# Splitting the sixteen-chunk layer-norm statistics of a macaron transformer layer into two halves of eight chunks

## The chip, the cores and the metric

The kernel runs on all 8 NeuronCores of one Trainium2 chip, each core with four of the 32 sequences and no exchange between cores. The metric is device time in microseconds (us) of the slowest core. The engines named below are TensorE (PE, its weight loads PEld), VectorE (DVE), ScalarE (ACT), GpSimd (POOL) and SyncE (SP); each works through its own list of instructions in order, and they meet through semaphores.

## The reference

Every sequence is a matrix of 2048 tokens by 1024 features and passes three residual stages, each of which starts with a layer norm without weights:

```
def _layernorm(x, axis=-1, eps=1e-5):
    m = jnp.mean(x, axis=axis, keepdims=True)
    v = jnp.var(x, axis=axis, keepdims=True)
    return (x - m) / jnp.sqrt(v + eps)

x = x + 0.5 * ffn(_layernorm(x), w_gate, w_up, w_down)   # silu(x wg^T) * (x wu^T), then wd^T; hidden 3072
x = x + attn(_layernorm(x), Wq, Wv, Wo, Wg, ...)         # q * ema_scan(v), a second norm, silu gate, Wo
x = x + 0.5 * ffn(_layernorm(x), w_gate, w_up, w_down)
```

The attention stage replaces softmax by a decaying sum over time per head, followed by a norm of its own with gamma and beta.

## The kernel before

One core runs its four sequences one after the other, and in each the phases A (feed-forward), B (attention) and C (the same feed-forward). A sequence stays on the chip as X, 16 chunks of 128 tokens by 1024 features in bf16. Each phase starts with `layer_norm_to_xn`, so the program passes through it 12 times.

The norm has three parts. `ln_stats(c)` takes one chunk's row sum on DVE (L541) and row sum of squares on ACT (L545), into one column of a small table STATS. It is called outside the norm: in A, after chunk c has received its feed-forward result (L680, the last third of the hidden dimension); in B, at the end of `part2(c)` (L853); at the change of sequence, after the next sequence's chunks have been loaded into X: `boundary_cb` stores four chunks and loads four (streams io0 to io3, on POOL), calls `ln_stats` for the four chunks before those, and the last four are called after phase C. Only the very first norm calls all sixteen itself. Then, once for all 16 chunks, come 18 small DVE instructions on 16 columns: mean (L552), its square (L555), variance (L558), and `emit_rsqrt`, an integer first guess of the inverse root and three Newton steps (L521 to L536). Each reads what the one in front of it wrote, and waits for it through DVE's own semaphore. Last, chunk by chunk: DVE subtracts and scales (L566, into one of two buffers TMPTM), PE transposes the result in eight 128x128 pieces into the one PSUM bank PSB7b (L570), ACT copies it to XN (L576). The matmuls that follow read XN: `L608` (gate) and `L635` (up) in A and C, `L718` (projections) in B.

The order on every engine is the order in which the Python code calls `em.op`; nothing reorders it later. `Em` derives the waits: every buffer or statistic has a key (such as `ST_ssum`), a reader waits for the key's last writer, a writer also for its readers, and a wait that an earlier one on the same engine already covers is left out.

Two things around the norm matter. Weights come over SP (stream `wl`): gate and up into WA and WB, later down (L653), and for attention four blocks (L693 to L703). In the first sequence the attention weights are first transposed by 32 DMA transposes (L454) with as many stores (L457), which stand on SP after the last L653 of phase A and ahead of L693. Inside attention `part1b` does the same 18 instructions for one chunk, on one column (L785 to L791, then L521 to L536); the change leaves that alone.

Of the kernel before, what the change touches and what calls it, by code (L numbers as in the profile page):

```python
# [11 lines left out]
ALU = mybir.AluOpType  # L12
AX = mybir.AxisListType
# [4 lines left out]
D = 1024  # L18
# [228 lines left out]
def build_program():  # L247
# [61 lines left out]
    STATS = sb("STATS", [128, 128], F32)  # L309
# [34 lines left out]
    em = Em()  # L344
# [14 lines left out]
    kX = [f"X{c}" for c in range(NCH)]  # L359
# [152 lines left out]
    def stat(namecol, c=None):  # L512
        base = st_cols[namecol]
        if c is None:
            return STATS[:, base:base + 16]
        return STATS[:, base + c:base + c + 1]

    MAGIC = 0x5f3759df

    def emit_rsqrt(varcol, varkey, wcol, wkey, tcol, tkey, zcol, zkey):  # L520
        em.op("vector", lambda v: v.tensor_scalar(wcol, varcol, float(EPS), None, ALU.add),  # L521
              reads=[varkey], writes=[wkey])
        wi, ti, zi = wcol.bitcast(I32), tcol.bitcast(I32), zcol.bitcast(I32)
        em.op("vector", lambda v: v.tensor_scalar(ti, wi, 1, None, ALU.arith_shift_right),
              reads=[wkey], writes=[tkey])
        em.op("vector", lambda v: v.tensor_scalar(zi, ti, -1, MAGIC, ALU.mult, ALU.add),
              reads=[tkey], writes=[zkey])
        for _ in range(3):
            em.op("vector", lambda v: v.tensor_tensor(tcol, zcol, zcol, ALU.mult),
                  reads=[zkey], writes=[tkey])  # L530
            em.op("vector", lambda v: v.tensor_tensor(tcol, tcol, wcol, ALU.mult),
                  reads=[tkey, wkey], writes=[tkey])
            em.op("vector", lambda v: v.tensor_scalar(tcol, tcol, -0.5, 1.5,
                                                      ALU.mult, ALU.add),
                  reads=[tkey], writes=[tkey])
            em.op("vector", lambda v: v.tensor_tensor(zcol, zcol, tcol, ALU.mult),  # L536
                  reads=[zkey, tkey], writes=[zkey])

    def ln_stats(c):
        xc = X[:, D * c:D * (c + 1)]  # L540
        em.op("vector", lambda v, xc=xc, c=c: v.reduce_sum(  # L541
            stat("ssum", c), xc, axis=AX.X), reads=[kX[c]], writes=["ST_ssum"])
        sq = TMPTM[:, D * (c % 2):D * (c % 2 + 1)]
        em.op("scalar", lambda s, xc=xc, c=c, sq=sq:
              s.activation(sq, xc, AF.Square, accum_out=stat("ssq", c)),  # L545
              reads=[kX[c]], writes=["ST_ssq", f"TT{c % 2}"])

    def layer_norm_to_xn(prestats=True):
        if not prestats:
            for c in range(NCH):  # L550
                ln_stats(c)
        em.op("vector", lambda v: v.tensor_scalar(  # L552
            stat("mu"), stat("ssum"), 1.0 / D, None, ALU.mult),
            reads=["ST_ssum"], writes=["ST_mu"])
        em.op("vector", lambda v: v.tensor_tensor(  # L555
            stat("musq"), stat("mu"), stat("mu"), ALU.mult),
            reads=["ST_mu"], writes=["ST_musq"])
        em.op("vector", lambda v: v.scalar_tensor_tensor(  # L558
            stat("var"), stat("ssq"), 1.0 / D, stat("musq"), ALU.mult, ALU.subtract),
            reads=["ST_ssq", "ST_musq"], writes=["ST_var"])  # L560
        emit_rsqrt(stat("var"), "ST_var", stat("sd"), "ST_sd",
                   stat("musq"), "ST_musq", stat("rstd"), "ST_rstd")
        for c in range(NCH):
            xc = X[:, D * c:D * (c + 1)]
            tm = TMPTM[:, D * (c % 2):D * (c % 2 + 1)]
            em.op("vector", lambda v, xc=xc, tm=tm, c=c: v.tensor_scalar(  # L566
                tm, xc, stat("mu", c), stat("rstd", c), ALU.subtract, ALU.mult),
                reads=[kX[c], "ST_mu", "ST_rstd"], writes=[f"TT{c % 2}"])
            bank, bkey = PSB7, "PSB7"
            items = [(lambda t, tm=tm, f=f, bank=bank: t.transpose(  # L570
                bank[:, 128 * f:128 * (f + 1)], tm[:, 128 * f:128 * (f + 1)], IDN[:]),
                [f"TT{c % 2}", "IDN"]) for f in range(KC)]
            em.group("tensor", items, writes=[bkey])
            xnv = XN[:].rearrange("p (f t) -> p f t", t=S)[:, :, 128 * c:128 * (c + 1)]
            bv = bank[:].rearrange("p (f t) -> p f t", t=128)
            em.op("scalar", lambda s, xnv=xnv, bv=bv: s.activation(xnv, bv, AF.Copy),  # L576
                  reads=[bkey], writes=[kXN[f][c] for f in range(KC)])

    def ffn_phase(tap=False, prestats=True, next_stats=True, tail_cb=None,
                  skip_gw0=False):  # L580
        layer_norm_to_xn(prestats=prestats)
        if tap:
            em.dma("st", lambda g: g.dma_start(out=dbg_xn, in_=XN[:]),
                   reads=[k for row in kXN for k in row], writes=["DBGXN"])
        nsl = NSLAB if DBG_SLABS is None else DBG_SLABS
        for j in range(nsl):
# [69 lines left out]
            for c in range(NCH):  # L656
# [20 lines left out]
                if j == NSLAB - 1 or (DBG_SLABS is not None and j == DBG_SLABS - 1):  # L677
                    xc = X[:, D * c:D * (c + 1)]
                    ac = ACC[:, D * c:D * (c + 1)]
                    em.op("vector", lambda v, xc=xc, ac=ac: v.tensor_tensor(  # L680
                        xc, xc, ac, ALU.add),
                        reads=[kX[c], kACC[c][0], kACC[c][1]], writes=[kX[c]])
                    if next_stats:
                        ln_stats(c)
                    if tail_cb is not None:
                        tail_cb(c)
# [3 lines left out]

    def attn_phase():
        layer_norm_to_xn(prestats=True)
        em.dma("wl", lambda s: s.dma_start(  # L693
            out=WA[:].rearrange("p (k h) -> p k h", h=D), in_=scr_a["wq"]),
# [131 lines left out]
        def part2(c):  # L826
# [15 lines left out]
            for n in range(2):  # L842
# [11 lines left out]
                    xc, xc, PSB[bank2][:], ALU.add),  # L854
                    reads=[kX[c], kPSB[bank2]], writes=[kX[c]])
            ln_stats(c)

        for c in range(NCH + 2):
# [21 lines left out]
    for w in ("wq", "wv", "wgt", "wo"):  # L880
# [5 lines left out]
        reads=[f"scrT_wgate_r{r}" for r in range(HID // 128)], writes=["WSLOTA"])  # L886
# [3 lines left out]
        reads=[f"scrT_wup_r{r}" for r in range(HID // 128)], writes=["WSLOTB"])  # L890
# [88 lines left out]
```

How the kernel before makes its waits and increments, by code:

```python
        def body(engobj, eng):  # L225
            waited = {}
            for inst in em.ins[eng]:
                for dep in inst["deps"]:
                    sem, val = resolve(dep)
                    key = id(sem)
                    if waited.get(key, 0) < val:
                        engobj.wait_ge(sem, val)
                        waited[key] = val
                bi = inst["fn"](engobj)
                if inst["stream"] is not None:
                    bi.then_inc(semh[("d", inst["stream"])], 16)
                elif inst["inc"]:
                    bi.then_inc(semh[("e", eng)], 1)
```

## Time and profile before

| what | us |
|---|---|
| median of the 8 runs shown | 7573.2 |
| lowest and highest of them | 7253.7 and 7932.08 |
| profiled execution, its own time | 7256.6 |
| its span (core 6, the slowest) | 7255.1 |
| spans of the 8 cores | 7231.1 to 7255.1 |
| PE busy | 5702.6 (79%) |
| DVE busy | 2082.8 (29%) |
| ACT busy | 1474.9 (20%) |

The page's busy shares are means over stages that differ: PE is nearly always busy in the feed-forward stages, waits in parts of attention, and stands between two phases while a norm is made ready. A change in the norm is therefore read in the stretch of a norm, by what PE waits for there.

### The profile page before, as it was taken

The numbers are of one execution on the slowest core, as the hardware profiler recorded it, in microseconds if no ns is written. First come the engines' busy times: TensorE is split into PE (matmuls) and PEld (weight loads), VectorE is DVE, ScalarE is ACT, GpSimd is POOL, SyncE is SP. The second block draws the span as 40 slices with busy tenths as digits, with TensorE's granted clock in tenths as the row PEclk, the third lists the DMA queues.
The fourth block names the chain that finished last, engine by engine and source line by source line (L and its number), as shares of the span: only waits on it lengthen the run. The fifth ranks groups of instructions, "written<-read, shape, count | busy, mean of one in ns | idle before, by whom it ended". The sixth has DMA issues, their size and how long they took to land.

```text
span 7255.1 us, 81111 instructions; the slowest of 8 cores (7231.1 to 7255.1 us)
## 1 busy us (share of the span) xinstructions
PE 5702.6 (79%) x29138; PEld 2833.1 (39%) x29138; DVE 2082.8 (29%) x3929; ACT 1474.9 (20%) x2342; POOL 173.1 (2%) x112
## 2 busy tenths in 40 slices
PE   0012998685998799786998799786998699786899
PEld 0011444443443344443443344443444344443444
DVE  0012124244123213344123213444123213444123
ACT  1000212222211211322211221322211221322211
POOL 0000000000000000000000000000000000000000
PEclk9999999787999899887999899887999799887899
DMA  8733013200013000100013110100012110100002
GB/s 98 117 97 94 24 47 85 67 1 24 30 41 99 30 35 24 47 1 24 24 47 86 37 41 24 47 1 24 24 45 73 45 47 24 47 1 24 24 35 70
DMA packets 152526, 322.12 MB, mean 44 GB/s; under 512 B 112336, under 2 KB 112336, under 8 KB 140048
## 3 DMA queue, kind: packets, MB, share of 16 engines
q1 hardware_dynamic: 134016, 239.10, 10.0%
q0 software_dynamic: 18128, 77.84, 6.3%
q8 instruction: 252, 4.13, 0.2%
q14 instruction: 130, 1.06, 0.0%
HBM read 291.74 MB, written 88.08 MB: 52 GB/s over the span
## 4 chain that ended last, share of the span: by engine, by line
PE 70%; DVE 9%; DMA 8%; issue 5%; ACT 4%; another core or an unknown queue 3%; DVEq 1%; SPq 0%; ACTq 0%; POOL 0%; POOLq 0%
PE PSB L608 18%; PE PSB L635 18%; PE PSB L660 14%; PE PSB L718 9%; PE PSB L846 5%; PE PSB7b L570 2%; ACT XN L576 2%; DMA TSTB<-nat_g 2%; DVE STATS L541 1%; DMA TSTB<-nat_u 1%; DVE ACC L674 1%; DMA X<-x 1%; DMA o<-X 1%; ACT ACC L839 1%
## 5 line engine op out<-in xcount | busy, mean ns | idle before, releaser
L645 DVE TENSOR_TENSOR H<-SG,PSB 128x512 bf16<-128x512 bf16 x768 | 528.1, 688 | 2620.6 <-PE PSB L635 2620.6
L660 PE MATMUL PSB<-WA,H 128*128 128x512 bf16 x4096 | 892.0, 380 | 32.0 <-DVE ACC L674 32.0
L625 ACT ACTIVATE SG<-PSB 128x512 bf16<-128x512 f32 x768 | 458.6, 597 | 2200.2 <-PE PSB L608 2200.1
L608 PE MATMUL PSB<-XN,WA 128*128 128x512 bf16 x4096 | 902.5, 383 | 0.0
L635 PE MATMUL PSB<-XN,WB 128*128 128x512 bf16 x4096 | 889.3, 379 | 0.0
L660 PEld LDWEIGHTS PSB<-WA,H 128*128 128x128 bf16 x4096 | 401.4, 98 | 520.1 <-issue 40.8
L608 PEld LDWEIGHTS PSB<-XN,WA 128*128 128x128 bf16 x4096 | 403.7, 99 | 491.7 <-issue 17.4
L635 PEld LDWEIGHTS PSB<-XN,WB 128*128 128x128 bf16 x4096 | 401.1, 98 | 482.9
L570 PE MATMUL PSB7b<-IDN,TMPTM 128*128 128x128 bf16 x1536 | 193.9, 305 | 489.8 <-ACT XN L576 269.0
L674 DVE SCALAR_TENSOR_TENSOR ACC<-PSB,ACC 128x512 bf16<-128x512 f32 x512 | 352.2, 690 | 349.9 <-PE PSB L660 347.1
L545 ACT ACTIVATE TMPTM<-X 128x1024 bf16<-128x1024 bf16 x192 | 202.8, 1056 | 1215.7 <-DMA X<-x 515.8
L608 PE MATMUL PSB<-XN,WB 128*128 128x512 bf16 x2048 | 444.6, 379 | 0.0
L635 PE MATMUL PSB<-XN,WA 128*128 128x512 bf16 x2048 | 444.6, 379 | 0.0
L660 PE MATMUL PSB<-WB,H 128*128 128x512 bf16 x2048 | 443.3, 379 | 0.0
L405 PE MATMUL PSB7b<-IDN,TSTB 128*128 128x128 bf16 x384 | 48.6, 306 | 476.2 <-DMA TSTB<-nat_g 349.7
L846 PE MATMUL PSB<-ACC 128*128 128x512 bf16 x1024 | 351.1, 518 | 87.3 <-ACT ACC L839 87.3
L576 ACT ACTIVATE XN<-PSB7b 128x1024 bf16<-128x1024 bf16 x192 | 196.8, 1025 | 805.1 <-PE PSB7b L570 805.1
L570 PEld LDWEIGHTS PSB7b<-IDN,TMPTM 128*128 128x128 bf16 x1536 | 148.2, 137 | 538.0 <-issue 538.0
L835 PE MATMUL PSB7b<-IDN,ACC 128*128 128x128 bf16 x512 | 63.5, 302 | 315.4 <-DVE ACC L831 315.4
L635 PEld LDWEIGHTS PSB<-XN,WA 128*128 128x128 bf16 x2048 | 200.6, 98 | 241.5
L660 PEld LDWEIGHTS PSB<-WB,H 128*128 128x128 bf16 x2048 | 200.4, 98 | 241.6
L608 PEld LDWEIGHTS PSB<-XN,WB 128*128 128x128 bf16 x2048 | 200.2, 98 | 241.8
(95 smaller groups left out, 4018.2 us busy)
## 6 DMA issues: line engine op xcount, KB each, us to landing
WA<-scr_g SPq DMA_DIRECT2D x16, 2048.0 KB, 8.4
WB<-scr_u SPq DMA_DIRECT2D x16, 2048.0 KB, 7.9
WA<-scr_d SPq DMA_DIRECT2D x16, 2048.0 KB, 7.6
o<-X POOLq DMA_DIRECT2D x16, 2048.0 KB, 8.4
X<-x POOLq DMA_DIRECT2D x16, 1024.0 KB, 12.0
WB<-scr_g SPq DMA_DIRECT2D x8, 2048.0 KB, 7.5
WA<-scr_u SPq DMA_DIRECT2D x8, 2048.0 KB, 7.5
WB<-scr_d SPq DMA_DIRECT2D x8, 2048.0 KB, 7.5
```

What stands on the lines that cost most here:

```text
L541: em.op("vector", lambda v, xc=xc, c=c: v.reduce_sum(stat("ssum", c), xc, axis=AX.X), reads=[kX[c]], writes=["ST_ssum"])
L545: s.activation(sq, xc, AF.Square, accum_out=stat("ssq", c)),
L570: items = [(lambda t, tm=tm, f=f, bank=bank: t.transpose(bank[:, 128 * f:128 * (f + 1)], tm[:, 128 * f:128 * (f + 1)], IDN[:]), [f"TT{c % ...
L576: em.op("scalar", lambda s, xnv=xnv, bv=bv: s.activation(xnv, bv, AF.Copy), reads=[bkey], writes=[kXN[f][c] for f in range(KC)])
L608: t.matmul(PSB[bank][:], wg_sl[:, SLAB * k + 128 * m:SLAB * k + 128 * (m + 1)], XN[:, S * k + 512 * g:S * k + 512 * (g + 1)], start=(k == ...
L625: s.activation(dst, PSB[bank][:], AF.Silu, scale=np32(1.0 / 127.0)),
L635: t.matmul(PSB[bank][:], wu_sl[:, SLAB * k + 128 * m:SLAB * k + 128 * (m + 1)], XN[:, S * k + 512 * g:S * k + 512 * (g + 1)], start=(k == ...
L645: v.tensor_tensor(dst, src0, PSB[bank][:], ALU.mult),
L660: t.matmul(PSB[bank][:], H[:, S * hc + 128 * c:S * hc + 128 * (c + 1)], wd_sl[:, D * hc + 512 * n:D * hc + 512 * (n + 1)], start=(hc == 0) ...
L674: v.scalar_tensor_tensor(dst, PSB[bank][:], SFIN, dst, ALU.mult, ALU.add),
L718: t.matmul(PSB[bank][:], XN[:, S * k + 128 * c:S * k + 128 * (c + 1)], wslot[:, D * k + 512 * n:D * k + 512 * (n + 1)], start=(k == 0), st ...
L846: t.matmul(PSB[bank2][:], Y2FM[sl][:, 128 * k:128 * (k + 1)], WOT[:, D * k + 512 * n:D * k + 512 * (n + 1)], start=(k == 0), stop=(k == KC ...
```

## The change

`STATS` is addressed in slices of eight columns. The 18 small instructions are emitted twice, first for chunks 0 to 7 and then for chunks 8 to 15, and the keys of the statistics are split the same way (`ST_ssum0` and `ST_ssum1`, and so on). The subtraction and scaling of chunk c now depends on its own half's keys. Its core (the keys of `mu`, `musq`, `var`, `sd` and `rstd` are all split as here):

```
-              reads=[kX[c]], writes=["ST_ssq", f"TT{c % 2}"])
+              reads=[kX[c]], writes=[f"ST_ssq{c // 8}", f"TT{c % 2}"])
...
-        em.op("vector", lambda v: v.tensor_scalar(
-            stat("mu"), stat("ssum"), 1.0 / D, None, ALU.mult),
-            reads=["ST_ssum"], writes=["ST_mu"])
...
-        emit_rsqrt(stat("var"), "ST_var", stat("sd"), "ST_sd",
-                   stat("musq"), "ST_musq", stat("rstd"), "ST_rstd")
+        for hb in range(2):
+            hs8 = slice(8 * hb, 8 * hb + 8)
+            em.op("vector", lambda v, hs8=hs8: v.tensor_scalar(
+                stat("mu", hs8), stat("ssum", hs8), 1.0 / D, None, ALU.mult),
+                reads=[f"ST_ssum{hb}"], writes=[f"ST_mu{hb}"])
...
+            emit_rsqrt(stat("var", hs8), f"ST_var{hb}", stat("sd", hs8), f"ST_sd{hb}",
+                       stat("musq", hs8), f"ST_musq{hb}", stat("rstd", hs8),
+                       f"ST_rstd{hb}")
         for c in range(NCH):
...
-                reads=[kX[c], "ST_mu", "ST_rstd"], writes=[f"TT{c % 2}"])
+                reads=[kX[c], f"ST_mu{c // 8}", f"ST_rstd{c // 8}"],
+                writes=[f"TT{c % 2}"])
```

Lines move: L541 becomes L543, L552 to L558 become L556 to L562, L521 to L536 become L523 to L538, L566 becomes L572.

On DVE, at the end of phase A, the list before had the last chunk's row sum, the 18 instructions and the normalisation of chunk 0; `se_vector` is DVE's own semaphore, `se_scalar` that of ACT, `se_tensor` that of PE (rows in between left out):

```order
L680 TENSOR_TENSOR X<-X,ACC 128x1024 [waits se_vector]
L541 TENSOR_REDUCE STATS<-X 128x1 [waits se_vector]
L552 TENSOR_SCALAR STATS<-STATS 128x16 [waits se_vector]
L555 TENSOR_TENSOR STATS<-STATS 128x16 [waits se_vector]
L558 SCALAR_TENSOR_TENSOR STATS<-STATS 128x16 [waits se_scalar,se_vector]
...
L536 TENSOR_TENSOR STATS<-STATS 128x16 [waits se_vector]
L566 TENSOR_SCALAR TMPTM<-X,STATS 128x1024 [waits se_vector]
L566 TENSOR_SCALAR TMPTM<-X,STATS 128x1024
L566 TENSOR_SCALAR TMPTM<-X,STATS 128x1024 [waits se_tensor,se_vector] x14
```

At the same place the list now has two chains of 18, one behind the other; here from the last instruction of the first chain on:

```order
L538 TENSOR_TENSOR STATS<-STATS 128x8 [waits se_vector]
L556 TENSOR_SCALAR STATS<-STATS 128x8
L559 TENSOR_TENSOR STATS<-STATS 128x8 [waits se_vector]
L562 SCALAR_TENSOR_TENSOR STATS<-STATS 128x8 [waits se_scalar,se_vector]
L523 TENSOR_SCALAR STATS<-STATS 128x8 [waits se_vector]
...
L535 TENSOR_SCALAR STATS<-STATS 128x8 [waits se_vector]
L538 TENSOR_TENSOR STATS<-STATS 128x8 [waits se_vector]
L572 TENSOR_SCALAR TMPTM<-X,STATS 128x1024 x2
L572 TENSOR_SCALAR TMPTM<-X,STATS 128x1024 [waits se_tensor,se_vector] x14
```

Both chains stand ahead of the first normalisation. Three instructions have lost their wait: the first of each chain (L556) and the normalisation of chunk 0 (L572).

At the change from the first sequence to the second the list of DVE now reads as follows; `sd_io2` and `sd_io3` are the loads of the third and the last four chunks of X:

```order
L687 TENSOR_TENSOR X<-X,ACC 128x1024 [waits se_vector]
L543 TENSOR_REDUCE STATS<-X 128x1 [waits sd_io2]
L543 TENSOR_REDUCE STATS<-X 128x1 [waits se_vector] x3
L543 TENSOR_REDUCE STATS<-X 128x1 [waits sd_io3,se_vector]
L543 TENSOR_REDUCE STATS<-X 128x1 [waits se_vector] x3
L556 TENSOR_SCALAR STATS<-STATS 128x8
L559 TENSOR_TENSOR STATS<-STATS 128x8 [waits se_vector]
```

The first chain, though it needs chunks 0 to 7 only, stands behind the row sums of chunks 12 to 15, as the one chain did before. The lists of PE, ACT, SP and POOL have as many rows as before, in the same order.

## Rows read from the trace of the kernel before

**Rows 1.** The page, parts 1 and 4: busy times and the chain.
```profile
PE 5702.6 (79%) x29138; PEld 2833.1 (39%) x29138; DVE 2082.8 (29%) x3929; ACT 1474.9 (20%) x2342; POOL 173.1 (2%) x112
PE 70%; DVE 9%; DMA 8%; issue 5%; ACT 4%; another core or an unknown queue 3%; DVEq 1%; SPq 0%; ACTq 0%; POOL 0%; POOLq 0%
```
**Rows 2.** Waits: who waited for whom: total us, times, longest us.
```profile
PE PSB7b L570 <- DVE TMPTM L566: 220.8, 12, 42.2
PEld PSB L718 <- issue: 41.9, 35, 32.6
PE PSB L718 <- DMA WB<-scr_wv: 32.4, 1, 32.4
PEld PSB L608 <- issue: 17.4, 63, 0.3
```
**Rows 3.** Timeline, third norm: start, length, engine, instruction, [idle before <-releaser].
```profile
1777.05 1.22 DVE L541 TENSOR_REDUCE STATS<-X 128x1 f32<-128x1024 bf16 x1
1778.01 0.19 ACT L545 ACTIVATION_READ_ACCUMULATOR TMPTM<-X 128x1 f32 x1
1778.38 0.17 DVE L552 TENSOR_SCALAR STATS<-STATS 128x16 f32<-128x16 f32 x1
1778.66 0.17 DVE L555 TENSOR_TENSOR STATS<-STATS 128x16 f32<-128x16 f32 x1
...
1783.13 0.18 DVE L536 TENSOR_TENSOR STATS<-STATS 128x16 f32<-128x16 f32 x1
1783.42 1.00 DVE L566 TENSOR_SCALAR TMPTM<-X,STATS 128x1024 bf16<-128x1024 bf16 x2
...
1784.11 1.01 PE L570 MATMUL PSB7b<-IDN,TMPTM 128*128 128x128 bf16 x8 [8.02 <-DVE TMPTM L566]
```
**Rows 4.** Groups by form: small DVE instructions; xcount | busy, mean ns.
```profile
L533 DVE TENSOR_SCALAR STATS<-STATS 128x1 f32<-128x1 f32 x204 | 31.3, 154 | 21.8
L536 DVE TENSOR_TENSOR STATS<-STATS 128x1 f32<-128x1 f32 x204 | 32.4, 159 | 21.3
L533 DVE TENSOR_SCALAR STATS<-STATS 128x16 f32<-128x16 f32 x36 | 6.3, 175 | 3.8
```
**Rows 5.** Timeline, DVE late in attention: one-column chain, and instructions without a wait.
```profile
1756.42 1.22 DVE L541 TENSOR_REDUCE STATS<-X 128x1 f32<-128x1024 bf16 x1
1757.56 0.68 DVE L766 TENSOR_TENSOR H<-PSB,H 128x512 bf16<-128x512 f32 x1
...
1760.81 0.15 DVE L785 TENSOR_SCALAR STATS<-STATS 128x1 f32<-128x1 f32 x1
...
1765.53 0.55 DVE L798 TENSOR_SCALAR ACC<-H,STATS 128x1024 bf16<-128x1024 bf16 x1
```
**Rows 6.** Timeline, SP and PE around the second norm.
```profile
1155.73 0.32 SPq L653 DMA_DIRECT2D WA<-scr_d  x1
1156.15 4.52 SPq L454 DMA_TRANSPOSE TSTB<-nat_wq  x1
...
1285.02 1.01 PE L570 MATMUL PSB7b<-IDN,TMPTM 128*128 128x128 bf16 x8 [1.62 <-ACT XN L576]
1318.44 6.23 PE L718 MATMUL PSB<-WB,XN 128*128 128x512 bf16 x16 [32.40 <-DMA WB<-scr_wv]
```
**Rows 7.** Timeline, row sums of the last four chunks at the three sequence changes.
```profile
2364.75 5.18 DVE L541 TENSOR_REDUCE STATS<-X 128x1 f32<-128x1024 bf16 x4 [23.36 <-DMA X<-x]
4005.89 5.19 DVE L541 TENSOR_REDUCE STATS<-X 128x1 f32<-128x1024 bf16 x4 [15.44 <-DMA X<-x]
5645.21 5.19 DVE L541 TENSOR_REDUCE STATS<-X 128x1 f32<-128x1024 bf16 x4 [13.13 <-DMA X<-x]
```
**Rows 8.** Timeline, PE: transposes of two successive chunks, fourth norm.
```profile
2375.77 1.01 PE L570 MATMUL PSB7b<-IDN,TMPTM 128*128 128x128 bf16 x8 [41.89 <-DVE TMPTM L566]
2378.26 1.01 PE L570 MATMUL PSB7b<-IDN,TMPTM 128*128 128x128 bf16 x8 [1.48 <-ACT XN L576]
```
**Rows 9.** Timeline, PE: first matmuls after a norm, longest and shortest.
```profile
2414.26 30.36 PE L608 MATMUL PSB<-XN,WA 128*128 128x512 bf16 x128
5694.34 28.73 PE L608 MATMUL PSB<-XN,WA 128*128 128x512 bf16 x128
2961.47 5.65 PE L718 MATMUL PSB<-WB,XN 128*128 128x512 bf16 x16
6240.23 4.68 PE L718 MATMUL PSB<-WB,XN 128*128 128x512 bf16 x16
```

More of the change, by code:

```diff
@@ L515, in stat @@
             return STATS[:, base:base + 16]
+        if isinstance(c, slice):
+            return STATS[:, base + c.start:base + c.stop]
         return STATS[:, base + c:base + c + 1]
@@ L541, in ln_stats @@
         em.op("vector", lambda v, xc=xc, c=c: v.reduce_sum(
-            stat("ssum", c), xc, axis=AX.X), reads=[kX[c]], writes=["ST_ssum"])
+            stat("ssum", c), xc, axis=AX.X), reads=[kX[c]], writes=[f"ST_ssum{c // 8}"])
         sq = TMPTM[:, D * (c % 2):D * (c % 2 + 1)]
@@ L551, in layer_norm_to_xn @@
                 ln_stats(c)
-        em.op("vector", lambda v: v.tensor_scalar(
-            stat("mu"), stat("ssum"), 1.0 / D, None, ALU.mult),
-            reads=["ST_ssum"], writes=["ST_mu"])
[L555 to L560, printed above, removed]
-        emit_rsqrt(stat("var"), "ST_var", stat("sd"), "ST_sd",
-                   stat("musq"), "ST_musq", stat("rstd"), "ST_rstd")
+        for hb in range(2):
[3 more added lines that the diff above has]
+                reads=[f"ST_ssum{hb}"], writes=[f"ST_mu{hb}"])
+            em.op("vector", lambda v, hs8=hs8: v.tensor_tensor(
+                stat("musq", hs8), stat("mu", hs8), stat("mu", hs8), ALU.mult),
+                reads=[f"ST_mu{hb}"], writes=[f"ST_musq{hb}"])
+            em.op("vector", lambda v, hs8=hs8: v.scalar_tensor_tensor(
+                stat("var", hs8), stat("ssq", hs8), 1.0 / D, stat("musq", hs8),
+                ALU.mult, ALU.subtract),
+                reads=[f"ST_ssq{hb}", f"ST_musq{hb}"], writes=[f"ST_var{hb}"])
+            emit_rsqrt(stat("var", hs8), f"ST_var{hb}", stat("sd", hs8), f"ST_sd{hb}",
+                       stat("musq", hs8), f"ST_musq{hb}", stat("rstd", hs8),
+                       f"ST_rstd{hb}")
         for c in range(NCH):
```

## The prediction

> **What bounds the kernel now.** The page first: PE is busy for 79% of the span and carries 70% of the chain that ended last, DVE 9% of it [rows 1]. DVE's 29% busy time says little, since its share of the chain comes in places where PE stands. The table of waits says where: PE's transposes of the norm (L570) waited for DVE's normalisation (L566) 12 times, once for each norm, 220.8 us in all [rows 2]. So whatever DVE does between the last statistic and the first normalisation is paid by PE.
>
> Next the timeline of one norm, the third [rows 3]. The last chunk's row sum runs on DVE from 1777.05 to 1778.27; ACT's sum of squares is read out by 1778.20, so ACT isn't late. The 18 small instructions then start at 1778.38 and the first normalisation at 1783.42, and PE, idle for 8.02 us, starts at 1784.11, released by that normalisation. From the end of the row sum (call it E) to the normalisation it is 5.15 us: 0.11 of wait, then 18 steps of (1783.42 − 1778.38)/18 = 0.280. An instruction takes 0.175 of each step [rows 4]; the rest is the wait for its predecessor.
>
> What follows must be exposed for a delay to count. After the transposes the feed-forward matmuls L608 start without waiting for anything but issue, at most 0.3 us [rows 2]. In attention, L718 waited for a DMA once, 32.4 us, behind the second norm [rows 2]: PE ends the transposes near 1286 and starts at 1318.44 on the arrival of WB [rows 6].
>
> **The change part by part.** Nothing is taken away from DVE's list but width: 18 instructions on 16 columns become 36 on 8 columns, and all 36 stand ahead of the first normalisation. I price the way from E to the first normalisation.
>
> Step of 8 columns: the trace of before has none. From one side there is the chain of one column in attention, (1765.53 − 1760.81)/18 = 0.262 per step [rows 5], from the other that of 16 columns, 0.280. In proportion to the columns, 7/15 of the way, a step of 8 is 0.2705 and an instruction 0.165 (between the mean 0.157 of the two one-column rows and 0.175) [rows 4]. Both ends are kept for the range; they lie close, so halving the width saves next to nothing.
>
> Hand-offs: three instructions no longer wait for the one in front of them: the first of each chain, and the normalisation of chunk 0, since the half that they need was finished earlier or is covered by a later wait. Such a place is in the trace: row sum L541 runs from 1756.42 to 1757.64, and the independent L766 behind it starts at 1757.56, 0.08 before that end [rows 5], not 0.11 after it. I take −0.08 for all three; the other end is a full step each, as if nothing were gained.
>
> Sum: the first chain starts at E − 0.08; 17 steps of 0.2705 bring its last instruction; the second chain starts 0.165 − 0.08 = 0.085 later; 17 more steps; the normalisation 0.085 after the last. E − 0.08 + 34 × 0.2705 + 2 × 0.085 = E + 9.29. Against 5.15 that is 4.14 us later in each norm.
>
> The Trainium skill has a rule that speaks against the gain at the hand-offs: VectorE: DVE Perf Modes, section "The DRAIN you can't avoid", says that the next instruction doesn't start until the pipe is empty and that leaving out semaphores between instructions buys nothing. By it each hand-off would be a full step: it is the second rival below. The same page of the Trainium skill, in "Two Vector instructions with no wait between them", lets an instruction that isn't held start earlier, which is what the overlap of 0.08 shows.
>
> Where it counts: at 11 of the 12 norms PE goes on with work that needs nothing else. At the second, the 4.14 us shorten the 32.4 us wait for WB to some 28, and cost nothing. The cover is SP's list, where 32 transposes start right behind the last L653 of phase A [rows 6]; that DMA waits on PE, so its start moves with the first norm's delay, which is therefore paid in full, while the second norm's own is hidden. If that cover were gone, it would be one more norm, 4.14.
>
> Nothing else moves. The split keys let the row sum and the square of chunk 8 go without waiting for chunk 7's; they wait for X itself in any case, so I put this at zero (between −0.1 us for one hand-off per norm, and none). ACT, PE, SP and POOL issue the same lists, and no DMA is added or passed. Behind the 36 instructions DVE holds back only the normalisations. From chunk 2 on these wait for PE and ACT, which take 2375.77 to 2378.26, 2.49 us, for a chunk [rows 8]; nothing of the delay is made up there, and chunk 8 finds its half long done.
>
> Total: 11 × 4.14 = 45.5. The sum is made against the profiled execution's own 7256.6 us (span 7255.1 and 1.5 around it): 7256.6 + 45.5 = 7302, or +0.63%. That execution lies at the lower end of the runs shown, 316.6 below their median of 7573.2, which takes in runs up to 7932.08; the forecast is for executions like the profiled one.
>
> Bounds: steps of 0.262 with an instruction of 0.157 give E − 0.08 + 34 × 0.262 + 2 × 0.077 = E + 8.98, so 3.83 × 11 = 42. Steps of 0.280 throughout and no gain at the hand-offs give 0.11 + 36 × 0.280 − 5.15 = 5.04, × 11 = 55. To this comes what the delays do to PE's clock, on which they could act either way: the first 128 matmuls after a feed-forward norm took between 28.73 and 30.36 us, the first 16 after an attention norm between 4.68 and 5.65 [rows 9], depending on when the clock rose from 1.2 to 2.4 GHz. Eight and three such places, each off by half of its spread, would move the sum by 8 × 0.8 + 3 × 0.5 = 8 us if all went one way; I count 0 and keep ±8 for the range.
>
> **The rivals.** First, the change does what its form suggests: the first half's work starts while the last chunks are still missing. The place is the sequence change, where DVE stands for 23.36, 15.44 and 13.13 us until the last four chunks of X have been loaded [rows 7]. Eight chunks' transposes take 8 × 2.49 = 19.9 us [rows 8]; in those gaps 19.9 + 15.4 + 13.1 = 48 us of them could run, and the time would be 7256.6 − 48 = 7208 at the three places, even if the other norms came out even. It decides from the point where the first chain stands ahead of the row sums that wait for `sd_io3`. Against it: the list shows it behind them, and DVE's rows in the timeline come in the list's order. 2 in 100.
>
> Second, the hand-offs gain nothing: 36 steps of 0.2705 and the wait of 0.11 make E + 9.85, 4.70 more than before, × 11 = 52, so 7308. For it: every small instruction in rows 3 starts 0.1 after its predecessor's end; against it, those all wait for the predecessor, and the row without a wait overlaps. 12 in 100.
>
> Third, the delay is covered: behind most norms something other than XN turns out to come last, as at the second one [rows 6]. If nine of the 12 were covered, 3 × 4.14 = 12 us would be left: 7269, no change that can be told. Against it: L608 shows no wait for a DMA, and L718 only that one [rows 2]. 4 in 100.
>
> Fourth, the later start of phases shifts the stores and loads of X among the eight cores. The wait for the last load runs from 13.13 to 23.36 us [rows 7]; with all three as long as the longest, 7.9 + 10.2 = 18 us are added: 7320. For it, only that the rows differ; against it, all cores shift alike. 4 in 100.
>
> **How the numbers follow.** The forecast, 7302, has 78 in 100. Its range and that of the second rival run from 7256.6 + 42 − 8, some 7290, to 7256.6 + 55 + 8, some 7320, and the fourth rival touches the end; 6 in 100 is left to the two cases below. About 0.2%, 14.5 us, is what a measurement of this kernel can tell from no change. Slower by more than that: 78 + 12 + 4 = 94. Within it: the third rival's 4. Faster: the first rival's 2.
>
> **What would show it.** In the timeline of a norm after the change: two chains of 18 on 8 columns, steps near 0.27, instructions near 165 ns; the first chain starting before the end of the last row sum, the second less than 0.1 after the last start of the first; first normalisation 9.3 us after E. In the waits: L570's total for DVE near 220.8 + 12 × 4.14 = 270, still 12 times, and L718's wait for WB near 28. It would be wrong if chains ran ahead of the last row sums, if an 8-column step came out below 0.26, or if the later part of a phase made the time up again.

## The result, and the profile after

The change makes the kernel slower: the ratio of its time to that of before is 1.0067, 95% interval 1.0056 to 1.0077, or 48.6 us on 7254. Six of its 11 runs compare, 7301.1 to 7306.0 us, with 15 of the 32 of before, 7251.6 to 7259.8; in the others the cores of one die, sometimes of both, were granted a lower clock and took up to 12% longer, so the medians over all runs, 7306.0 and 7419.9, can't be set side by side.

The profiled execution of the changed kernel took 7331.8 us, 26 more than the median. Its cores say why not to compare it as it stands:

```profile
core 0: 7282.9 us, clock 0.918
core 3: 7294.8 us, clock 0.917
core 7: 7330.2 us, clock 0.912
die 0 (median of its cores): 7288.3 us, clock 0.918
die 1 (median of its cores): 7314.1 us, clock 0.914
```

Core 7, the slowest, lost its time in the first feed-forward stage. The fences show the granted clock there, first of core 7, then of core 3, last of core 5, which is on core 7's die (columns: stretch, length, busy time and count of PE, PEld, DVE, ACT and POOL, PEclk, DMA share, GB/s):

```profile
800.00:900.00 100.00, 100.00 (x383) 41.44 (x381) 15.14 (x22) 15.30 (x26) 0.00 (x0) 0.81 0.11 43
900.00:1000.00 100.00, 100.00 (x405) 42.44 (x403) 8.25 (x12) 22.91 (x39) 0.00 (x0) 0.86 0.06 22
```

```profile
800.00:900.00 100.00, 100.00 (x465) 45.35 (x464) 13.76 (x20) 22.72 (x38) 0.00 (x0) 1.00 0.11 43
900.00:1000.00 100.00, 100.00 (x465) 45.37 (x464) 11.00 (x16) 25.12 (x42) 0.00 (x0) 1.00 0.06 22
```

```profile
800.00:900.00 100.00, 100.00 (x465) 45.34 (x464) 13.06 (x19) 23.32 (x39) 0.00 (x0) 1.00 0.11 43
```

With PE busy all the time, 383 matmuls fit into 100 us at 0.81 and 465 at 1.00. Cores 6 and 7 were below 1.00 from about 745 to 970 us, the other six were not. The change doesn't touch the matmuls of that stage. So what follows is read on core 3, which was not held back there in either kernel's profile: 7250.0 us before, 7294.8 after. The mean of its die's four cores went up by 46.9 us.

The timeline of the third norm on core 3, to be laid beside [rows 3]:

```profile
1785.62 1.22 DVE L543 TENSOR_REDUCE STATS<-X 128x1 f32<-128x1024 bf16 x1
1786.57 0.19 ACT L547 ACTIVATION_READ_ACCUMULATOR TMPTM<-X 128x1 f32 x1
1786.75 0.16 DVE L556 TENSOR_SCALAR STATS<-STATS 128x8 f32<-128x8 f32 x1
1787.02 0.17 DVE L559 TENSOR_TENSOR STATS<-STATS 128x8 f32<-128x8 f32 x1
1787.29 0.17 DVE L562 SCALAR_TENSOR_TENSOR STATS<-STATS 128x8 f32<-128x8 f32 x1
1787.56 0.17 DVE L523 TENSOR_SCALAR STATS<-STATS 128x8 f32<-128x8 f32 x1
1788.02 0.17 DVE L526 TENSOR_SCALAR STATS<-STATS 128x8 int32<-128x8 int32 x1 [0.29 <-DVE STATS L523]
...
1791.57 0.17 DVE L538 TENSOR_TENSOR STATS<-STATS 128x8 f32<-128x8 f32 x1
1791.66 0.17 DVE L556 TENSOR_SCALAR STATS<-STATS 128x8 f32<-128x8 f32 x1
...
1796.31 0.17 DVE L538 TENSOR_TENSOR STATS<-STATS 128x8 f32<-128x8 f32 x1
1796.39 1.00 DVE L572 TENSOR_SCALAR TMPTM<-X,STATS 128x1024 bf16<-128x1024 bf16 x2
1797.08 1.01 PE L577 MATMUL PSB7b<-IDN,TMPTM 128*128 128x128 bf16 x8 [12.43 <-DVE TMPTM L572]
```

The reader is to see four things. The row sum ends at 1786.84 and the first chain starts at 1786.75, before that end. The second chain follows the last instruction of the first by 0.09, the normalisation that of the second by 0.08. In between the steps are 0.27. And PE, which waited 8.02 us here before (8.04 on core 3), waits 12.43, released by the normalisation. One step is longer than the others: from L523 to L526 it is 0.46. Over the 12 norms the way from the end of the row sum to the normalisation is 9.37 to 9.38 us in three, 9.56 to 9.57 in eight and 9.69 in one, on average 9.53; before, it was 5.15 to 5.16 and once, with one such longer step, 5.33.

Two waits of core 3 sum it up (total us, times, longest), first before the change, then after it:

```profile
PE PSB7b L570 <- DVE TMPTM L566: 212.2, 12, 40.3
PE PSB L718 <- DMA WB<-scr_wv: 33.5, 1, 33.5
```

```profile
PE PSB7b L577 <- DVE TMPTM L572: 263.6, 12, 43.8
PE PSB L725 <- DMA WB<-scr_wv: 26.9, 1, 26.9
```

PE waits 51.4 us longer for DVE at the norms. At the second norm it gets the delay of 4.4 us back from the wait for the weight block, which shrank by 6.6; where the other 2.2 come from is not shown.

### The profile page after: what moved, and what is told of

Same layout as the page of the kernel before. It is cut to its first block, busy times and chain, and to the rows that moved or that the text cites. A ratio compares the mean times of both kernels' runs of the same rounds, so it can differ in the third digit from the quotient of the medians.

```text
span 7330.2 us, 81506 instructions; the slowest of 8 cores (7282.9 to 7330.2 us)
## 1 busy us (share of the span) xinstructions
PE 5750.1 (78%) x29138; PEld 2843.8 (39%) x29138; DVE 2115.2 (29%) x4145; ACT 1474.8 (20%) x2342; POOL 173.1 (2%) x112
## 4 chain that ended last, share of the span: by engine, by line
PE 70%; DVE 9%; DMA 7%; issue 5%; ACT 4%; another core or an unknown queue 3%; DVEq 1%; SPq 0%; ACTq 0%; POOL 0%; POOLq 0%
PE PSB L615 18%; PE PSB L642 18%; PE PSB L667 15%; PE PSB L725 9%; PE PSB L853 5%; PE PSB7b L577 2%; ACT XN L583 2%; DMA TSTB<-nat_g 2%; DMA TSTB<-nat_u 1%; DVE STATS L543 1%; DVE ACC L681 1%; ACT ACC L846 1%; ACT TMPTM L790 1%; PE PSB7b L842 1%
## 5 line engine op out<-in xcount | busy, mean ns | idle before, releaser
L667 PE MATMUL PSB<-WA,H 128*128 128x512 bf16 x4096 | 912.9, 386 | 26.3 <-DVE ACC L681 26.3
L642 PE MATMUL PSB<-XN,WB 128*128 128x512 bf16 x4096 | 901.3, 383 | 0.0
L615 PE MATMUL PSB<-XN,WB 128*128 128x512 bf16 x2048 | 449.6, 382 | 0.0
L583 ACT ACTIVATE XN<-PSB7b 128x1024 bf16<-128x1024 bf16 x192 | 196.6, 1024 | 857.4 <-PE PSB7b L577 857.4
```

The source lines that it names most:

```text
L615: t.matmul(PSB[bank][:], wg_sl[:, SLAB * k + 128 * m:SLAB * k + 128 * (m + 1)], XN[:, S * k + 512 * g:S * k + 512 * (g + 1)], start=(k == ...
L642: t.matmul(PSB[bank][:], wu_sl[:, SLAB * k + 128 * m:SLAB * k + 128 * (m + 1)], XN[:, S * k + 512 * g:S * k + 512 * (g + 1)], start=(k == ...
L667: t.matmul(PSB[bank][:], H[:, S * hc + 128 * c:S * hc + 128 * (c + 1)], wd_sl[:, D * hc + 512 * n:D * hc + 512 * (n + 1)], start=(hc == 0) ...
```

## The experiments

Ratios are to the kernel before, run on the same chip in the same session, with 95% intervals; 0.1% is 7.3 us. Traces are those of core 3. The times of the four chains, of the old chain twice and of the early halves at the sequence changes rest on two runs each.

**Interleaving the two chains.** The theory of the prediction is that dependent steps in a row set the price; the rivals are the number of instructions and the split keys themselves. The recorded pairs of the two halves are emitted alternately:

```
+        lists = []
+        real_op = em.op
         for hb in range(2):
+            rec = []
+            em.op = lambda *a, rec=rec, **k: rec.append((a, k))
...
+            lists.append(rec)
+        em.op = real_op
+        for ops in zip(*lists):
+            for a, k in ops:
+                em.op(*a, **k)
```

> The same 36 instructions on 8 columns as in the change, but the two chains are emitted alternately (first instruction of each, second of each, and so on). Theory (the price is the number of dependent steps in a row, 0.27 us each, and an independent instruction follows its neighbour after 0.09): the second chain fits into the waits of the first, the way from the end of the last row sum to the first normalisation is 18 x 0.27 + 0.1 = about 5.0 us against 5.16 before and 9.4 to 9.6 after, so the time is that of before, 7254, within 5 us. Rival (the price is the number of instructions, whatever they wait for): still 36 x 0.27, about 9.5 us, and 7303. Rival (the split keys or the wider table of waits cost something elsewhere): 7303 as well, with a short way.

Ratio 1.0015 (0.9978 to 1.0053): no difference from before that can be told. The interval is wide, but it ends below that of the change, 1.0056 to 1.0077. The trace decides. Its third norm, each row here a pair of instructions, one of either half:

```profile
1780.06 0.36 DVE L560 TENSOR_SCALAR STATS<-STATS 128x8 f32<-128x8 f32 x2
1780.73 0.27 DVE L563 TENSOR_TENSOR STATS<-STATS 128x8 f32<-128x8 f32 x2 [0.30 <-DVE STATS L560]
1781.00 0.34 DVE L566 SCALAR_TENSOR_TENSOR STATS<-STATS 128x8 f32<-128x8 f32 x2
1781.28 0.34 DVE L523 TENSOR_SCALAR STATS<-STATS 128x8 f32<-128x8 f32 x2
...
1785.39 1.00 DVE L581 TENSOR_SCALAR TMPTM<-X,STATS 128x1024 bf16<-128x1024 bf16 x2
```

Both instructions of a pair fit into one step of 0.27 to 0.28 (the first row has a longer one), since the second needs nothing of the first. The way to the normalisation is 4.88 to 5.32 us in the 12 norms, as with one chain. The same 36 instructions with the same keys cost nothing when their waits overlap: it was the order that cost, neither their number nor the keys.

**Four chains.** The keys and slices go by `c // 4`, `for hb in range(4)`, `hs8 = slice(4 * hb, 4 * hb + 4)`.

> Four chains on 4 columns, one behind the other, instead of two on 8. Theory: 4 x 17 steps of 0.266 and four hand-offs of 0.09, with the odd longer step about 18.6 us from the row sum to the first normalisation, 13.5 more than before in each of 11 norms: 7254 + 148 = 7402. Rival (the cost goes by columns handled, which are 16 as ever): 7254 to 7303, no more than the change itself.

Ratio 1.0208 (1.0178 to 1.0237), 151 us. The way is 18.74 to 18.96 us, 13.7 longer than before, times 11 is 151. The price goes by the number of steps, and hardly by their width.

```profile
PE PSB7b L577 <- DVE TMPTM L572: 379.0, 12, 54.7
```

This wait is 166.8 us above the 212.2 of before, 12 times 13.9.

**The old chain twice.** In the kernel before:

```
+        for rep in range(2):
+            em.op("vector", lambda v: v.tensor_scalar(
+                stat("mu"), stat("ssum"), 1.0 / D, None, ALU.mult),
...
```

> The kernel before, with its chain of 18 instructions on all 16 columns emitted twice in a row (the second computes the same values again). No split keys, no halves. Theory: 36 steps of 0.28, 10.2 us from the row sum to the first normalisation, 5.05 more than before: 7254 + 11 x 5.05 = 7310. Rival (the change's loss comes from the halves and their keys, not from the length of the chain): 7254.

Ratio 1.0080 (1.0051 to 1.0110), 58 us. The way is 10.00 to 10.37 us, 4.98 longer than before on average, times 11 is 55; no halves are needed to lose the time. It is 0.6 longer than the change's: 34 steps that are 0.007 wider make 0.24, and the two waits that stay, at the first chain and at the normalisation, 0.19 each.

**The cover of the second norm.** The same loop with `range(1 + extra)`, and `extra=5` in the first sequence's attention only.

> The kernel before, with five further chains on 16 columns at the second norm only (first sequence, before attention), where PE afterwards waits some 28 to 33 us for a weight block. Five chains are 5 x 5.0 = 25 us. Theory (the wait covers them): the time stays at 7254 within 5 us, and the wait for the block falls to 3 to 9 us. Rival (the block's arrival moves with the norm, or something else there is late): up to 25 us more, 7279.

Ratio 1.0001 (0.9986 to 1.0015). The way at that norm is 29.93 us, 24.8 more than before, and the time doesn't move. The wait for the block gave way (this core's granted clock was 0.885 here and 0.919 before, so the verdict rests on the times):

```profile
PE PSB L719 <- DMA WB<-scr_wv: 9.5, 1, 9.5
```

So the second norm's own delay is hidden, and 11 norms are the right count.

**Halves put to use at the sequence changes.** The chains and the chunks become functions; for the norm after phase C the first half is emitted ahead of the row sums of the last four chunks, the other nine norms keep one chain on 16 columns:

```
             if s + 1 < SEQS:
+                chain(0)
+                for k in range(8):
+                    norm_chunk(k)
                 for i in range(4):
                     ln_stats(12 + i)
```

> The halves are put to use at the three sequence changes: after phase C's last chunk the chain of chunks 0 to 7 and their normalisation and transposes are emitted ahead of the row sums of chunks 12 to 15, the chain of chunks 8 to 15 behind them; the other nine norms keep one chain on 16 columns. Theory (the order of emission decides; DVE then works through chunks 0 to 7 while the last chunks of X are loaded): the first matmul after the norm comes 10 to 19 us earlier at each of the three places, some 40 us in all, 7254 - 40 = 7214 (7205 to 7235). Rival (the normalisation of the early chunks holds up DVE, PE or ACT as long as it saves): 7254.

Ratio 0.9931 (0.9907 to 0.9955), 50 us faster. The first sequence change:

```profile
2350.76 0.16 DVE L552 TENSOR_SCALAR STATS<-STATS 128x8 f32<-128x8 f32 x1
...
2356.37 1.01 PE L593 MATMUL PSB7b<-IDN,TMPTM 128*128 128x128 bf16 x8 [14.70 <-DVE TMPTM L588]
...
2370.74 5.18 DVE L543 TENSOR_REDUCE STATS<-X 128x1 f32<-128x1024 bf16 x4
...
2381.17 0.17 DVE L558 SCALAR_TENSOR_TENSOR STATS<-STATS 128x8 f32<-128x8 f32 x1 [4.71 <-ACT TMPTM L547]
```

In front of the last four row sums DVE now waits 1.1 us at most; on core 3 it stood there for some 20 us at each change before (13 to 23 on the core of [rows 7]). PE transposes eight chunks in that time. This is the first rival's mechanism, at about the first rival's price of 48 us, and it needs the order that the change doesn't have. On core 3 the stretches with the three changes, each from the norm ahead of phase C to the attention norm of the next sequence, got shorter by 18.8, 14.3 and 16.7 us. Part of the gap is lost again: as the last row shows, the second chain waits 3.5 to 4.7 us for ACT's squares of the last chunks, which stand behind the copies of the early chunks in ACT's list.

**The same in attention.** Chain 0 is emitted after `part2(7)`, one normalisation in each of the last eight rounds:

```
             if c < NCH:
                 part1a(c)
+            if c >= 10:
+                norm_chunk(c - 10)
...
+            if c == 9:
+                chain(0)
```

> The halves are put to use between attention and phase C: the chain of chunks 0 to 7 is emitted after chunk 7 has left attention, their normalisation and transposes one by one in the last eight rounds of the attention loop; chunks 8 to 15 follow as usual; the other eight norms keep one chain on 16 columns. Theory: eight chunks' transposes, 8 x 2.49 = 20 us, leave the stretch in which PE waits, in four norms, less what chain and transposes cost inside attention (up to 5 us for the chain and 1 to 2 us for a round): 7254 - 4 x 10 to 18 = 7180 to 7215. Rival (attention's own chain from PE over DVE and ACT takes on each early chunk in full, 2.5 us each): 7254.

Ratio 1.0036 (1.0022 to 1.0051): 26 us slower, not 40 to 75 faster. A round of the attention loop, 27.2 to 27.5 us before (row sums of two successive chunks), takes 30.6 to 32.8 in six of the eight rounds where a normalisation was put in; the two short ones at the end hardly change. One such round, and behind it the same place in the kernel before, where L783 is the square:

```profile
3324.00 0.60 ACT L781 ACTIVATE H<-PSB 128x512 bf16<-128x512 f32 x1 [1.13 <-PE PSB L754]
3327.26 0.61 PE L593 MATMUL PSB7b<-IDN,TMPTM 128*128 128x128 bf16 x8
3327.97 1.02 ACT L599 ACTIVATE XN<-PSB7b 128x1024 bf16<-128x1024 bf16 x1 [3.37 <-PE PSB7b L593]
3328.89 1.05 ACT L819 ACTIVATE TMPTM<-H 128x1024 bf16<-128x1024 bf16 x1
3330.20 0.16 DVE L827 SCALAR_TENSOR_TENSOR STATS<-STATS 128x1 f32<-128x1 f32 x1 [10.00 <-ACT TMPTM L819]
```

```profile
3303.81 0.60 ACT L745 ACTIVATE H<-PSB 128x512 bf16<-128x512 f32 x1 [1.13 <-PE PSB L718]
3304.30 1.05 ACT L783 ACTIVATE TMPTM<-H 128x1024 bf16<-128x1024 bf16 x1
```

ACT's copy to XN (L599) waits 3.37 us for transposes that PE reaches after its projections. The square of attention's own norm (L819), which could have run at 3324.6, stands behind that copy in ACT's list, starts 4.3 us later, and DVE's chain waits for it.

**Both.** The last two together.

> Both of the last two: early halves at the three sequence changes and in the four attention stages. Theory: the gains add, since the places lie apart: 7254 - 80 to 110 = 7145 to 7175. Rival: one of the two gives nothing, then the time of the other alone.

Ratio 0.9971 (0.9955 to 0.9987), 21 us faster: −50 and +26 add up. The time expected was missed, since it counted on a gain in attention.

**The copy behind the square.** Only ACT's copy is moved:

```
             if c >= 10:
-                norm_chunk(c - 10)
+                norm_chunk(c - 10, copy=False)
             if c >= 1:
                 part1b(c - 1)
+            if c >= 10:
+                xn_copy(c - 10)
```

> As the run with early halves in attention alone, but ACT's copy of the transposed chunk into XN is emitted behind part1b, so that in ACT's list it stands after the attention norm's square and not before it. Theory (what made that run slow is that the copy, which waits for PE's transposes at the end of the projections, held up the square behind it by some 4 us in six rounds of each attention stage): the square starts again when the last gate projection has been read, the round falls back from 31 to some 27.5 us, and the 20 us that leave the norm of phase C are kept: 7257 - 4 x 14 to 19 = 7180 to 7205. Rival (PE's transposes or DVE's extra instruction make the round long): again some 7285.

Ratio 0.9890 (0.9866 to 0.9914), 80 us faster, more than expected. The square now runs ahead of the transposes and the copy, and the round is 26.9 to 28.0 us:

```profile
3272.23 1.05 ACT L824 ACTIVATE TMPTM<-H 128x1024 bf16<-128x1024 bf16 x1
3274.99 0.61 PE L593 MATMUL PSB7b<-IDN,TMPTM 128*128 128x128 bf16 x8
3275.70 1.02 ACT L604 ACTIVATE XN<-PSB7b 128x1024 bf16<-128x1024 bf16 x1 [2.33 <-PE PSB7b L593]
```

**Both, with the copy behind.**

> The last run's attention with the early halves at the three sequence changes as well. Theory: the gains add, 50 us to those of the last run: 7130 to 7155. Rival: if the attention part still costs time, some 7235 as with both before.

Ratio 0.9822 (0.9805 to 0.9840), 129 us faster than before, and so, by the two ratios, some 180 faster than the change, with the same two halves. The gains add (50 and 80).

## Why the prediction was right, and where it was not

**The step that failed is the base of the number**: "The sum is made against the profiled execution's own 7256.6 us". The prediction meant its forecast for "executions like the profiled one"; how many are like it, and what the others take, it left out of the sum and of the range, and its ±8 us for the clock covered only what the delays do to it. The runs showed something else in its place: of the changed kernel's 11 runs six took 7301 to 7306 us, inside 7290 to 7320, and five took 7584 to 8187; of the 32 of before, 15 took 7252 to 7260 and 17 took 7356 to 8143. The profiled execution, 7331.8, lies outside the range too, with cores 6 and 7 at a clock of 0.81 for some 220 us in a stage whose matmuls the change doesn't touch. Set beside the median shown then, 7573.2, the bare 7302 even looks like a gain of 3.6%, and only the words and the chances say that it is a loss of 0.63%. The runs of before that were shown, 7253.7 to 7932.08, should have warned of it. What carries over is the ratio, 1.0063, which the measured 1.0067 bears out; a single time should have been tied to it.

**What bounds a norm** held: PE waits for the first normalisation at all 12 norms. On core 6, which the prediction had read, the total went from 220.8 to 271.0 us, where 270 was worked out; on core 3 it grew by 51.4 against 12 × 4.14 = 49.7.

**The step of 8 columns** held: 0.273 in the trace, 0.2705 taken; an instruction takes 0.163 to 0.172, 0.165 taken. The four chains and the doubled one follow the same price.

**The hand-offs** held: 0.08 to 0.09 before the end of the one in front, at all three places, but for one normalisation of the 12, which starts 0.23 after that end. The second rival, a full step each, is refuted: without its wait an instruction starts some 0.19 us earlier. The Trainium skill, VectorE: DVE Perf Modes, "The DRAIN you can't avoid", says that leaving out semaphores between DVE instructions saves nothing. The trace disagrees here. The section after it in the Trainium skill, "Two Vector instructions with no wait between them", by which only an instruction that is held has to wait until all earlier ones have finished, agrees with the trace.

**The sum** was 0.24 us per norm short, 9.29 against 9.53, the one term that was mis-sized: 0.09 of it because 34 steps are 0.273 and not 0.2705, and 0.15 on average because eight of the 12 ways have one step that is 0.18 to 0.19 too long and a ninth has one that is 0.31 too long. 11 × 0.24 is 2.6, so 48 in place of 45.5, and 48.6 was measured.

**The eleventh part**, that the second norm costs nothing, is shown by the five further chains there. The wait for the weight block fell from 32.4 to 25.4 us on core 6, further than to the 28 of the prediction.

**The loads of X** were rightly left at zero: on core 3 the last row sums waited 19.7 to 20.1 us for them before and 18.3 to 19.1 after, so the longer waits of the fourth rival don't show there.

**The first rival** was rightly set aside, as the trace shows both chains behind the last row sums. With the order that it needs the three places gave 50 us against its price of 48, but that its sum is so close is partly luck: its three parts, 19.9, 15.4 and 13.1, differ from the 18.8, 14.3 and 16.7 of core 3, and the second chain's wait for ACT was not in them.

My own theory fell once, in attention: I expected the early chunks to cost 1 to 2 us a round there, and overlooked what stood behind the copy on ACT. The run with the copy moved settles that this was the cause.

## What to carry to other kernels

Splitting a piece of work in two gains nothing until the first part is also emitted earlier, ahead of what it doesn't need; on an engine that works in order, dependencies that were made finer but stand at the same place only lengthen the list. A chain of tiny dependent instructions is paid by the step, not by width: keep it as one wide chain, or interleave independent ones. When a piece is moved forward, look on every engine that it uses at the instruction directly behind it, since a wait that it brings along holds that one up too.

## What the runs showed of the hardware

A DVE instruction that waits for the one in front starts 0.10 to 0.11 us after its end, one without a wait 0.08 to 0.09 before its end, about 0.19 us between them where an instruction itself takes 0.17.

In nine of the 12 norms one step was 0.18 to 0.31 us longer than the others of its kind, at the same place of the list on all eight cores (for the third norm after the fourth instruction, for the sixth after the 26th), so it goes with the place in the program and not with the moment. Counted over all rows that core 3's trace has for DVE, those of waits and semaphores too, the number of the instruction behind the longer step, counted from 0, is each time a multiple of 128 plus 59 or 60: the nine lie 640, 1024, 2432, 640, 640, 1791, 641 and 1024 rows apart. The three norms whose chains hold no such place have no longer step. In the kernel before one norm's chain holds such a place, and that is the one with 5.33 us. So a longer chain also meets such places more often; what happens there is not shown.

The clock of 0.81 over 100 us of nothing but matmuls is neither of the two levels 1.2 and 2.4 GHz. The Trainium skill, TensorE: Matmul & The Clock Gate, "Part 1: The HAM clock gate", tells of a limit of 13/16 for a whole die once three of its cores run dense matmuls, held while the load lasts. The figure, 0.8125, fits that row, but the rest differs here: only two of the die's cores showed it, and only for part of a stage in which all of them ran matmuls.
